# Attention and convolution block: the row of score maxima turned by one VectorE transpose and laid by eight DMAs, with a shorter lead before the first scores

## The reference

```python
hid = _group_norm(xr, norm_w, norm_b)                     # xr: [16, 128, 1024]
qkv = einsum('oc,bcl->bol', qkv_w, hid) + qkv_b
weight = einsum('bhct,bhcs->bhts', q * scale, k * scale)  # 8 heads of 16 channels
weight = softmax(weight, axis=-1)
a = einsum('bhts,bhcs->bhct', weight, v)
x = x + (einsum('oc,bcl->bol', proj_w, a) + proj_b)
...
h = gelu(rmsnorm2d(x, norm1_w)); x = x + conv1x1(h, conv_w, conv_b)
h = gelu(conv1x1(rmsnorm2d(x, norm2_w), ffn_w1, ffn_b1)); x = x + conv1x1(h, ffn_w2, ffn_b2)
```

## Time and profile before

| | |
|---|---|
| median of 3 runs | 1763.99 us (1761.72 to 1764.31) |
| profiled execution, its own time | 1763.75 us |
| its span, first to last instruction | 1761.8 us |
| PE busy | 1698.3 us, 96% |
| DVE busy | 1492.8 us, 85% |
| ACT busy | 1366.5 us, 78% |
| POOL busy | 335.7 us, 19% |
| attention with all engines at work | about 75 us to 1455 us of the span |

### The profile page before, as it was taken

One profiled execution on the slowest core, in us unless ns is written; L12 is line 12 of the kernel. 1 busy time (PEld: TensorE's weight loads), 2 busy tenths in 40 slices (PEclk: granted clock), 3 DMA queues, 4 the chain that ended last, 5 costly groups with the idle time before them and its releaser, 6 DMA issues.

```text
span 1761.8 us, 33312 instructions
## 1 busy us (share of the span) xinstructions
PE 1698.3 (96%) x12402; PEld 693.2 (39%) x12402; DVE 1492.8 (85%) x2606; ACT 1366.5 (78%) x2480; POOL 335.7 (19%) x411
## 2 busy tenths in 40 slices
PE   3999999999999999999999999999999997699999
PEld 2333333333333333333333333333333332355555
DVE  4899999999999999999999999999999992455552
ACT  1288888888888888888888888888888887466664
POOL 4101111111111111111111111111111011322220
PEclk8599999999999999999999999999999999799999
DMA  5422323232323132324242324141313011233341
GB/s 111 64 44 52 61 41 71 46 66 43 70 40 73 40 72 38 76 37 75 36 76 37 76 36 76 33 67 35 67 35 66 10 21 38 79 104 110 107 109 72
DMA packets 61121, 106.18 MB, mean 60 GB/s; under 512 B 27296, under 2 KB 30112, under 8 KB 60960
## 3 DMA queue, kind: packets, MB, share of 16 engines
q1 hardware_dynamic: 58656, 95.66, 27.6%
q10 hardware_dynamic: 2304, 8.39, 1.2%
HBM read 34.48 MB, written 9.06 MB: 25 GB/s over the span
## 4 chain that ended last, share of the span: by engine, by line
PE 83%; DVE 11%; issue 2%; SPq 1%; DMA 1%; POOL 1%; ACT 1%; DVEq 0%; ACTq 0%; POOLq 0%
PE psum L607 26%; PE psum L578 25%; PE psum L591 10%; DVE maxes L865 9%; PE psum L673 6%; PE psum L561 4%; PE psum L645 2%; PE psum L647 2%; PE psum L646 2%; PE psum L549 2%; PE psum L514 2%; PE psum L690 1%; DVE stats L881 1%; DVE rows L849 1%; SPq L309 0%
## 5 line engine op out<-in xcount | busy, mean ns | idle before, releaser
L865 DVE TENSOR_REDUCE maxes<-psum 128x1 f32<-128x512 f32 x2048 | 1269.5, 680 | 92.3 <-PE psum L578 90.8
L779 ACT ACTIVATE probs<-psum 128x512 f32<-128x512 f32 x2048 | 1107.4, 600 | 219.2 <-PE psum L591 196.6
L578 PE MATMUL psum<-k_stack,q_stack 62*128 62x512 f32 x2048 | 785.6, 461 | 19.0 <-DVE maxes L865 8.9
L591 PE MATMUL psum<-q_stack,k_stack 64*128 64x512 f32 x2048 | 770.8, 455 | 1.2 <-ACT probs L779 1.1
L607 PE MATMUL psum<-probs,values 128*32 128x256 f32 (+1 forms) x6912 | 621.2, 431 | 0.5 <-ACT probs L779 0.5
L578 PEld LDWEIGHTS psum<-k_stack,q_stack 62*128 62x128 f32 x2048 | 329.5, 188 | 561.8 <-DVE maxes L865 445.7
L591 PEld LDWEIGHTS psum<-q_stack,k_stack 64*128 64x128 f32 x2048 | 318.7, 185 | 14.8 <-ACT probs L779 10.5
L607 PEld LDWEIGHTS psum<-probs,values 128*32 128x32 f32 x6912 | 136.2, 108 | 286.8 <-issue 228.7
L673 PE MATMUL psum<-probs,inv_den 128*128 128x512 f32 x256 | 116.5, 598 | 0.0
L411 POOL CAST parts<-neg_max 128x16 fp32r<-128x16 f32 x64 | 12.6, 196 | 538.2 <-DVE neg_max L841 538.2
L788 ACT ACTIVATE probs<-psum,params_sb 128x512 f32<-128x512 f32 x128 | 82.5, 685 | 20.6 <-PE psum L647 14.2
(11 more groups left out here) (82 smaller groups left out, 1044.6 us busy)
## 6 DMA issues: line engine op xcount, KB each, us to landing
q_stack<-q_high SPq DMA_DIRECT2D x256, 64.0 KB, 2.2
k_stack<-k_high SPq DMA_DIRECT2D x128, 128.0 KB, 4.0
x_sb<-in_x SPq DMA_DIRECT2D x16, 512.0 KB, 5.2
q_stack<-q_low SPq DMA_DIRECT2D x128, 64.0 KB, 4.0
k_stack<-k_low SPq DMA_DIRECT2D x64, 128.0 KB, 4.3
attn<-raw SPq DMA_DIRECT2D x128, 64.0 KB, 2.3
inv_den<-inv_den_rows SPq DMA_DIRECT2D x128, 64.0 KB, 2.3
values<-inv_rms_rows SPq DMA_DIRECT2D x16, 512.0 KB, 5.0
```

The source lines that it names most:

```text
L578: nc.tensor.matmul(psum[:, BANKS + tile % BANKS, :], q_stack[used, place, chunk // 4, p, 128 * (chunk % 4):128 * (chunk % 4) + 128], k_sta ...
L591: nc.tensor.matmul(psum[:, tile % BANKS, :], k_stack[used, place, p, 128 * chunk:128 * chunk + 128], q_stack[used, place, t, p, :], start= ...
L779: nc.scalar.activation(probs[:, tile % 8, :], psum[:, tile % BANKS, :], ACT.Exp, scale=SCALE).then_inc(probs_ready, 1)
L865: nc.vector.tensor_reduce(maxes[:, chunk // 4, j, 4 * p + chunk % 4, key_half:key_half + 1], psum[:, BANKS + max_tile(u, s, k) % BANKS, :] ...
```

## The change

There are three edits. `turn_half` issues one transpose over 128 partitions instead of four of 32 partitions; each block of 32x32 is turned in its place, so `rows` becomes 128 partitions by 32. Because a query's maxima of one half unit then lie on four groups of 16 partitions, `maximum_rows` issues eight DMAs, each of 16 pieces of 128 bytes, instead of two of 16 pieces of 512 bytes each, and `ROW_DMAS`, by which the waits on `rows_in` count, goes from 2 to 8. And the lead is reached otherwise: ten maximum steps are made before the first scores instead of thirteen, and each of the first three steps with scores makes two maximum steps, so that from the fourth on the lead is 13 as before.

```diff
-LEAD = 13
+LEAD, START = 13, 10
-STACK_DMAS, ROW_DMAS, HEAD_DMAS, WEIGHT_DMAS = 18, 2, 8, 6
+STACK_DMAS, ROW_DMAS, HEAD_DMAS, WEIGHT_DMAS = 18, 8, 8, 6
-        rows = sb("rows", [32, 128], fp32r)
+        rows = sb("rows", [128, 32], fp32r)
+        def max_items(u, s):
+            at = u * STEPS + s
+            caught_up = LEAD - START
+            if at < 0:
+                items = [at + START]
+            elif at < caught_up:
+                items = [START + 2 * at, START + 2 * at + 1]
+            else:
+                items = [at + LEAD]
+            return [divmod(g, STEPS) for g in items if g >= 0]
...
             def maximum_rows(v, t):
-                    sp.dma_start(row.rearrange("n (k f) -> n k f", f=128),
-                                 rows[16 * j:16 * j + 16, :].bitcast(fp32)).then_inc(rows_in, 16)
+                    for q in range(4):
+                        of = 32 * q + 16 * j
+                        sp.dma_start(row.rearrange("n (k f) -> n k f", f=128)[:, :, 32 * q:32 * q + 32],
+                                     rows[of:of + 16, :].bitcast(fp32)).then_inc(rows_in, 16)
...
             # PE, slot()
+                    *ahead, (unit, step) = [(-1, 0)] + max_items(u, s)
+                    for extra in ahead[1:]:
+                        for k in range(4):
+                            maximum_scores(*extra, k)
                     for k in range(4):
-                        maximum_scores(u, s, k)
+                        maximum_scores(unit, step, k)
...
             # DVE
-                for q in range(4):
-                    last = nc.vector.transpose(
-                        rows[:, 32 * q:32 * q + 32].bitcast(fp32),
-                        parts[32 * q:32 * q + 32, :, :, :].rearrange("q j n c -> q (j n c)").bitcast(fp32))
-                last.then_inc(rows_ready, 1)
+                nc.vector.transpose(rows[:, :].bitcast(fp32),
+                                    parts[:, :, :, :].rearrange("q j n c -> q (j n c)").bitcast(fp32)).then_inc(rows_ready, 1)
...
                 for s in steps_of(part):
-                    take_maxima(u, s)
+                    for item in max_items(u, s):
+                        take_maxima(*item)
```

More of the change, by code:

```diff
@@ L271, in run, with max_tile @@
                 refine(c)
[L273 to L279, removed]
+        def max_items(u, s):
[8 more added lines that the diff above has]
+            return [divmod(g, STEPS) for g in items if g >= 0]
+        def max_tile(unit, step, k):
+            return unit * TILES + 4 * step + k
         def image_of_x(b, lo=0, n=PIXELS):
@@ L566, in wait_for_bank, with maximum_scores @@
                 at_least(pe, freed, tile - BANKS + 1)
-            def maximum_scores(u, s, k):
-                unit, step = max_item(u, s)
+            def maximum_scores(unit, step, k):
                 place = unit % RING
@@ L572, in maximum_scores @@
                     return
-                j, key_half, p, chunk, tile = k % 2, k // 2, step % 2, step // 2, max_tile(u, s, k)
+                j, key_half, p, chunk, tile = k % 2, k // 2, step % 2, step // 2, max_tile(unit, step, k)
                 used = slice(ROWS * j, ROWS * j + MAX_ROW)
@@ L847, in turn_half, with take_maxima @@
                 at_least(dve, rows_in, n * (16 * ROW_DMAS))
-                for q in range(4):
-                    last = nc.vector.transpose(
-                        rows[:, 32 * q:32 * q + 32].bitcast(fp32),
-                        parts[32 * q:32 * q + 32, :, :, :].rearrange("q j n c -> q (j n c)").bitcast(fp32))
-                last.then_inc(rows_ready, 1)
-            def take_maxima(u, s):
-                unit, step = max_item(u, s)
+                nc.vector.transpose(rows[:, :].bitcast(fp32),
+                                    parts[:, :, :, :].rearrange("q j n c -> q (j n c)").bitcast(fp32)).then_inc(rows_ready, 1)
+            def take_maxima(unit, step):
                 half_unit = NT * unit + step // NK
@@ L861, in take_maxima @@
                         j, key_half, p, chunk = k % 2, k // 2, step % 2, step // 2
-                        dve.wait_ge(max_ready, max_tile(u, s, k) + 1)
+                        dve.wait_ge(max_ready, max_tile(unit, step, k) + 1)
                         if step % NK == 0 and k == 0:
@@ L865, in take_maxima @@
                         nc.vector.tensor_reduce(maxes[:, chunk // 4, j, 4 * p + chunk % 4, key_half:key_half + 1],
-                                                psum[:, BANKS + max_tile(u, s, k) % BANKS, :],
+                                                psum[:, BANKS + max_tile(unit, step, k) % BANKS, :],
                                                 axis=AX.X, op=ALU.max).then_inc(max_taken, 1)
```

## The result

The changed kernel took 1777.98 us in the median (four runs, 1773.66 to 1782.46) against 1763.63 us for the kernel before in the same comparison: a ratio of 1.0083, 95% interval 1.0057 to 1.0110, or 14.3 us. The profiled execution took 1782.46 us with a span of 1780.4 us; it is the slowest of the four, so its waits are probably somewhat above the typical.

The account below looks back on a forecast made before the run. It took PE to bound half 0, VectorE a quarter of half 1, and SP to be late in half 0 of fourteen images. 1763.75 - 7.0 (transpose) + 24.1 (rows) + 1.5 (start) gave 1782 us, range 1759 to 1794.

Parts of the forecast that it names:

- What bounds: PE's chain in half 0, a quarter VectorE's in half 1; SP late at 14 of 64 turns, in half 0.
- The transpose: Each turn on VectorE: 0.21 us instead of 0.83, saving 0.54 us at step 5 of thirteen half 1 slots, -7.0 us.
- The rows: Eight row DMAs, serial on SP at 0.67 us each, make PE wait around half 0 in fourteen images: +24.1 us.
- The start: Before and during the first scores: scores 1.2 us earlier, but leftover maximum tiles delay the fourth step: +1.5 us.
- one of the rivals: "The clock comes later": PE's pause before the first scores prolongs half clock, 1783 to 1786 us; 0.15 within the main case.
- The sum: Whole kernel: 1763.75 - 7.0 + 24.1 + 1.5 = 1782.35 us, stated as 1782 us.
- Even: Rival: waits for rows only about 0.5 us an image, total 1762 to 1767 us; chance 0.13.
- In time: Rival: row DMAs issue quicker, SP catches up in half 0, only the saving stays: 1755.5 to 1758.3 us; chance 0.13.
- Transposes in series: Rival: the 128-partition transpose takes 0.83 us, so nothing is saved and turns come later: 1799 us; chance 0.03.
- small pieces land late: Rival: 128-byte pieces take twice 1.9 us to land, lengthening waits after the turns: 1839 us; chance 0.03.

Follow-up runs that it names:

- the pair with START 13: Changed kernel with thirteen maximum steps before the first scores, 1779.84 us, and the same with half 0's next rows issued ahead of the stack DMAs, 1757.85 us.
- START 13: Changed kernel with thirteen maximum steps before the first scores again, single transpose and eight row DMAs kept: 1779.84 us, ratio 1.0100 against the kernel before.
- one transpose alone: Kernel before with one 128-partition transpose into an unread tile and two row DMAs from zeros, maxima not subtracted: 1749.81 us, ratio 0.9930.
- the order in SP's list: Changed kernel with the next unit's rows issued ahead of the 18 stack DMAs in half 0: 1760.44 us, ratio 0.9992 against the kernel before.
- the larger dose: Changed kernel with START 13 and ten stack DMAs moved from half 1 into half 0, ahead of the rows: 1922.63 us, ratio 1.0908 against the kernel before.

## Why the prediction was right, point by point

**What bounds.** SP late in half 0 of fourteen images, with slack of its own elsewhere: this held. Undoing only the order took 17.5 us away (16 by the ratios), and 22 us in the pair with START 13.

**The transpose.** Its duration was right (201 ns). Its worth was the term most mis-sized: -7.0 us predicted, -12.6 measured (-9.9 to -14.8 by the interval). I counted the step right behind the turn of step 4 in half 1. In the profiles that step has 7.9 us of the saving over fourteen images, where I had 7.0; the other steps of half 1 have 2.9 us more, half 0, which I had put at nothing, has 1.1, and about 1 us is saved before unit 1.

**The rows.** The start-to-start time (0.67 taken) is (747.14 to the last issue at 751.77) / 7 = 0.66 us; the landing after the last issue, 1.67 us in the chain below, was taken as 1.9:

```profile
741.95 1.92 SPq L317
743.91 0.59 SPq L317
...
751.12 0.61 SPq L329
751.77 1.67 DMA q_stack<-rows
```

The waits came to 17.0 + 5.8 = 22.9 us, against 24.1 predicted. That they came so near is in part luck: of the three images that I worked out the seventh has 2.1 us (1.95 predicted), but the first has 4.1 (2.52) and the last 1.8 (0.70), while the other eleven have 1.35 on average.

The edit costs more than these waits: 30.0 us by START 13 against one transpose alone. In the profiles of that pair the waits are 22.2 us, and the steps right behind them (step 8, and steps 0 and 1 of the next half) are 6.1 us longer, nearly all of it in the three images in which the clock falls. That is the term that I left out, since I had looked for a clock effect at the start only. With the four transposes kept, the rows begin later and the waits are longer, 29.7 us, with 3.7 behind them, of 31.0 lost. In the changed kernel, after a wait of 2.6 us at the end of half 0:

```profile
1104.00:1111.00 7.00, 5.16 (x35) 1.69 (x31) 5.07 (x9) 4.28 (x8) 2.00 (x2) 1.00 0.21 43
1111.50:1118.00 6.50, 6.24 (x33) 2.42 (x37) 3.07 (x5) 3.82 (x8) 0.00 (x0) 0.50 0.01 1
```

TensorE was busy for 5.16 of 7 us, and then its clock was granted at the lower level. The step that began the next slot took 4.32 us instead of 2.48. There are four such stretches in this profile, of 3 to 7 us, in the first, third, eleventh and last of the fourteen images; before there was none between 84 and 1489 us.

**The start.** +1.5 predicted, +2.3 measured alone (0.7 to 3.9). The mechanism held, the fourth step 2.8 us later within the -1.2 to 3.1 given; in the profile of the order in SP's list, with the same start, it is 4.2 us later, outside of it. There the clock came later, as one of the rivals had it, and in the changed kernel's own profile it didn't: full from 84.0 us on, against 83.3 before.

**The sum.** +18.6 us predicted over the profiled execution's own time, +14.3 measured in the medians; the terms measured alone give -12.6 + 30 + 2.3 = +20, and the profiled execution has +18.7. Two errors of opposite sign, 5.6 us too little saving and 6 us left out behind the waits, nearly cancel; that the sum came this near is luck, while its direction and its main term are not.

**The rivals.** "Even" fails by the waits, 1.6 us an image instead of 0.5. "In time" fails with 0.66 us from start to start against the 0.57 it needed. "Transposes in series" fails by the 201 ns, and "small pieces land late" by the 1.67 us. By the second, the exemption of transfers inside SBUF that the Trainium skill makes (DMA: Bandwidth & Descriptors, Why small descriptors are slow) agrees with the trace: the last DMA of 128-byte pieces landed after 1.67 us, no later than the 1.9 us of the earlier trace rows. Its advice in Rules for kernel authors of the same page, to coalesce many small transfers, held here too, but by the issuing queue and not by bandwidth: the page of either kernel has a mean of 60 GB/s.

## What to carry to other kernels

Price an added DMA on the queue that issues it: here 0.66 us each, in series with whatever stands behind it in the list, while the data itself hardly matters. A list with idle time on average can be full in one stretch; look for the waits that a queue does not have, here 14 of 64. Before giving up an edit that overfills such a stretch, move issues that nobody needs soon out of it: one transpose with eight DMAs costs 1.0% in one order of SP's list and gains 0.6% in another, both with START 13.

## What the runs showed of the hardware

A single DMA issue on SP, as a rule 0.59 us, now and then takes 1 to 2 us (1.92 us at 741.95 in the chain above). This was hidden before; once SP is on the path, such an issue can lengthen the wait. In the first, eleventh and last of the fourteen images, whose last step of half 0 is lengthened most (by 3.64, 3.09 and 1.80 us), three issues of half 0 took over 1 us, in the third, whose step 7 is lengthened most (by 1.95), four, in the others at most two. This probably also spreads the runs from 1773.66 to 1782.46, where the four of the kernel before lie within 3 us; that isn't shown. I didn't find what makes an issue long; the kernel before has them too, 46 of 1250 over 0.8 us.

Short pauses of TensorE can cost more than their length. In the profiles of the changed kernel, of the same with START 13 and of the eight row DMAs alone, TensorE's waits for rows within the fourteen images were 0.2 to 3.2 us long. The ten of 1.27 us or more, and none of those of 1.18 us or less, had the granted clock at the half at their end or within 2 us behind it, for 3 to 7 us. In the larger dose the clock fell in the course of each of the fourteen waits of 8.6 to 11.1 us, for 10 to 14 us. This is what these profiles show; no run varied the length of a pause by itself.
